# Attention with gated low-rank experts: orders in the slot of new weights, and probabilities of one or two key blocks written by four DMAs and read by one

## The reference

```python
xn = layernorm(x)
q = rmsnorm((xn @ Wq.T) as 32 heads of 128) * q_norm_w
k = rmsnorm((xn @ Wk.T) as 8 heads of 128) * k_norm_w
v = (xn @ Wv.T) as 8 heads of 128
scores = q @ k.T / sqrt(128)                 # 4 q heads share one k and v head
bias = where(rel > 0, -1e30, slope * rel)    # causal, with slopes by head
out = softmax(scores + bias) @ v
s = out @ Wo.T
g = silu(sum over 8 experts of the low-rank products, weighted by a softmax router)
y = x + s * g
```

## Time and profile before

| | |
|---|---|
| time, median of 3 runs | 741.79 us (741.38 to 743.2) |
| the profiled execution's own time | 743.02 us |
| its span in the trace | 741.2 us |
| TensorE busy | 720.8 us, 97% |
| VectorE, ScalarE, GpSimd busy | 600.6, 559.7, 335.6 us |
| DMA | 148.02 MB, mean 200 GB/s |
| granted TensorE clock | 0.998 |

### The profile page before, as it was taken

One profiled execution on the slowest core, in us unless ns is written; L12 is line 12 of the kernel. 1 busy time (PEld: TensorE's weight loads), 2 busy tenths in 40 slices (PEclk: granted clock), 3 DMA queues, 4 the chain that ended last, 5 costly groups with the idle time before them and its releaser, 6 DMA issues.

```text
span 741.2 us, 14630 instructions
## 1 busy us (share of the span) xinstructions
PE 720.8 (97%) x3741; PEld 605.4 (82%) x3741; DVE 600.6 (81%) x1490; ACT 559.7 (76%) x1440; POOL 335.6 (45%) x320
## 2 busy tenths in 40 slices
PE   8899999999999999999999999999999999999997
PEld 7787878878788888888888888888888887888776
DVE  6857798678886889787986889777986979878985
ACT  4566888587877877777886978778887768769873
POOL 4223434454434543545444543346326434445556
PEclk9999999999999999999999999999999999999999
DMA  8015968687685778868686786958787785867761
GB/s 304 1 30 140 274 170 235 194 239 224 172 267 160 223 203 229 242 158 254 183 231 198 229 241 173 280 141 232 214 229 217 191 264 147 232 196 204 205 191 72
DMA packets 214773, 148.02 MB, mean 200 GB/s; under 512 B 48992, under 2 KB 205536, under 8 KB 214624
## 3 DMA queue, kind: packets, MB, share of 16 engines
q1 hardware_dynamic: 184224, 130.39, 60.7%
q10 hardware_dynamic: 30528, 17.38, 8.9%
HBM read 85.84 MB, written 61.87 MB: 199 GB/s over the span
## 4 chain that ended last, share of the span: by engine, by line
PE 62%; DMA 10%; DVE 9%; issue 7%; ACT 6%; SPq 2%; POOL 2%; ACTq 1%; DVEq 0%; POOLq 0%
PE out_ps L1363 6%; PE qkv_ps L1363 5%; PE out_ps L1365 5%; PE qkv_ps L1364 5%; PE out_ps L1364 5%; PE qkv_ps L1365 5%; DMA x_sb<-turning 5%; PE score_ps L1363 4%; PE score_ps L1365 3%; PE score_ps L1364 3%; PE mix_ps L1363 3%; PE mix_ps L1365 3%; PE mix_ps L1364 3%; DMA turning<-squared 3%; PE turn_ps L1364 2%
## 5 line engine op out<-in xcount | busy, mean ns | idle before, releaser
L589 POOL TENSOR_TENSOR pt_lo<-x_sb,pt_hi 128x512 fp32r<-128x512 f32 x129 | 164.2, 1296 | 257.5 <-ACT pt_hi L795 257.5
L720 ACT ACTIVATE probs<-probs,neg_max 128x128 f32<-128x128 f32 (+3 forms) x256 | 142.1, 559 | 33.3 <-DVE neg_max L1018 32.1
L1018 DVE CUSTOM_DVE_ANT_0 probs<-score_ps,cst,slope 128x128 f32<-128x128 f32 (+3 forms) x256 | 131.0, 543 | 20.0 <-PE score_ps L1365 19.1
L728 ACT ACTIVATE probs<-probs,recip 128x128 f32<-128x128 f32 (+3 forms) x252 | 126.1, 549 | 8.0 <-DVE recip L1025 8.0
L795 ACT ACTIVATE pt_hi<-x_sb 128x512 fp32r<-128x512 f32 x153 | 86.6, 623 | 50.6 <-issue 31.7
L1363 PE MATMUL qkv_ps<-w_hi,xt_hi 128*128 128x256 f32 (+1 forms) x364 | 118.8, 326 | 2.4 <-DVE xt_lo L961 1.5
L1364 PE MATMUL qkv_ps<-w_lo,xt_hi 128*128 128x256 f32 (+1 forms) x364 | 118.4, 325 | 0.0
L1365 PE MATMUL qkv_ps<-w_hi,xt_lo 128*128 128x256 f32 (+1 forms) x364 | 118.0, 324 | 0.0
L1363 PE MATMUL out_ps<-wo_hi,o_hi 128*128 128x512 f32 x252 | 102.5, 407 | 0.8 <-DVE o_lo L1063 0.6
L1039 DVE STREAM_TRANSPOSE squared<-probs 128x256 f32<-128x256 f32 (+3 forms) x124 | 100.4, 810 | 0.1
L579 POOL TENSOR_TENSOR inv_rms<-sums,minus_half 128x5 f32<-128x5 f32 x64 | 76.9, 1202 | 50.1 <-DVE sums L1077 50.1
(11 more groups left out here) (203 smaller groups left out, 1630.3 us busy)
## 6 DMA issues: line engine op xcount, KB each, us to landing
qk_moved<-turning_qk SPq DMA_DIRECT2D x60, 320.0 KB, 3.4
turning_qk<-qk_squared ACTq DMA_DIRECT2D x212, 80.0 KB, 2.2
turning<-squared SPq DMA_DIRECT2D x120, 128.0 KB, 2.4
x_sb<-turning SPq DMA_DIRECT2D x30, 512.0 KB, 5.2
w_raw<-wqkv SPq DMA_DIRECT2D x32, 384.0 KB, 5.0
turning<-squared SPq DMA_DIRECT2D x120, 96.0 KB, 2.1
x_sb<-turning SPq DMA_DIRECT2D x30, 384.0 KB, 4.2
turning<-squared SPq DMA_DIRECT2D x128, 64.0 KB, 2.0
```

The lines of the kernel that those rows point to most:

```text
L589: nc.gpsimd.tensor_tensor(by_quad(pt_lo, j), moved_block(t, j), by_quad(pt_hi, j).bitcast(F32), ALU.subtract).then_inc(pt_lo_by_pool, 1)
L720: nc.scalar.activation(probs[:, h, 0:n], probs[:, h, 0:n], ACT.Exp, bias=neg_max[:, h:h + 1], scale=-1.0, accum_out=total[:, h:h + 1]).the ...
L728: nc.scalar.activation(to[:, h, 0:n], probs[:, h, 0:n], ACT.Copy, scale=recip[:, h:h + 1]).then_inc(probs_ready, 1)
L1018: nc.vector.tensor_tensor_reduce(probs[:, h, 0:n], score_bank(t, h), cst[:, C_DIST + SEQ - n:C_DIST + SEQ], slope[:, h:h + 1], HUGE, ALU.a ...
```

## The change

Four orders change, and one way through DRAM.

TensorE's `project_new` takes chunks 0 to 2 first, with `w_hi` and then with `w_lo`, and then chunk 3 with both; before, all four chunks with `w_hi` came first. The part of VectorE for the same slot (`w_slot`) makes the third `w_lo` ahead of the second reciprocals, and `turned_qk_lo` (q_lo and k_lo of the next unit) ahead of the first `square_probs`. The latter two are exchanged in slot t = 2 of the prologue too, there alone. In the last group's slot 5, GpSimd makes its block of `pt_lo` of unit 3 ahead of `inverse_rms`, as it did in the other groups.

The probabilities of a unit with one or two key blocks are laid out without a gap between the two pairs of heads, written by four DMAs once both pairs are there, and read by one. Units with three or four key blocks are moved as before. The counts that others wait for (`WRITTEN`, `MOVED`) follow.

```diff
-WRITTEN = counter([16 * QUADS] * BLOCKS)
-MOVED = counter([32] * BLOCKS)
+WRITTEN = counter([16 * QUADS] * BLOCKS), counter([0, 0, 16 * QUADS, 16 * QUADS] * BATCH)
+MOVED = counter([16, 16, 32, 32] * BATCH)
...
+        squared_whole = squared[:, :, :, :].rearrange("p k s n -> p k (s n)")
...
+        def moved_whole(t):
+            return moved[t % 2].rearrange("p q s n -> p q (s n)")[:, :, 0:keys_of(t) * P]
+
         def moved_block(t, j):
+            if keys_of(t) <= 2:
+                return moved_whole(t).rearrange("p q (s n) -> p q s n", s=2)[:, :, :, j * P // 2:(j + 1) * P // 2]
             return moved[t % 2][:, :, :, j * P // 2:(j + 1) * P // 2]
...
             def move(g, t, u, soon=False):
...
+                if keys_of(t) <= 2:
+                    if soon and u is not None:
+                        sp.wait_ge(qk_lo_ready, K_AND_Q_LO(g, u, 0))
+                        read_qk(g, u)
+                    write_all_probs(g, t)
+                    if u is not None and not soon:
+                        read_qk(g, u)
+                    sp.wait_ge(probs_written[0], WRITTEN[0](g, t, 16 * QUADS))
+                    sp.dma_start(moved_whole(t), turning[t % 2, :, :, 0:2 * n].rearrange("q p n -> p q n")).then_inc(probs_moved, 16)
+                    return
                 write_probs(g, t, 0)
...
+            def write_all_probs(g, t):
+                n = keys_of(t) * P
+                sp.wait_ge(probs_squared, TWO(g, t, 2))
+                for q in range(QUADS):
+                    sp.dma_start(turning[t % 2, q, :, 0:n].rearrange("(k r) n -> r k n", k=QUADS),
+                                 squared_whole[q * QUAD:(q + 1) * QUAD, :, 0:n]).then_inc(probs_written[0], 16)
...
@@ gpsimd, slot
-                if t % BLOCKS == W_SLOT and here(t + 3, left):
+                if t % BLOCKS == W_SLOT:
                     turned_lo(g, t - 2)
                 if here(t + 2, left):
                     inverse_rms(g, t + 2)
                 if t % BLOCKS == W_SLOT and here(t + 3, left):
                     split_w(g + 1, range(W_DVE, KC))
-                elif t % BLOCKS == W_SLOT:
-
-                    turned_lo(g, t - 2)
...
@@ vector, w_slot
                 reciprocals(g, t, 0)
+                split_w(g + 1, range(W_DVE - 1, W_DVE))
                 reciprocals(g, t, 2)
-                split_w(g + 1, range(W_DVE - 1, W_DVE))
                 normalize_q(g, t + 2)
                 square_both(g, t + 2)
+                turned_qk_lo(g, t + 1)
                 square_probs(g, t, 0)
-                turned_qk_lo(g, t + 1)
                 square_probs(g, t, 2)
...
@@ vector, slot
+                if t == 2:
+
+                    turned_qk_lo(g, t + 1)
                 if here(t, left):
                     square_probs(g, t, 0)
-                if here(t + 1, left):
+                if here(t + 1, left) and t > 2:
                     turned_qk_lo(g, t + 1)
...
@@ tensor, project_new
+                first, last = range(0, KC - 1), range(KC - 1, KC)
+                for chunks in (first, last):
+                    for to, cols, _ in parts:
+                        if chunks is first and to is parts[1][0]:
+                            pe.wait_ge(k_norm_ready, ONE(g, t - 1, 1))
+                            pe.wait_ge(v_lo_ready, ONE(g, t - 1, 1))
+                        for c in chunks:
                             pe.wait_ge(w_hi_done, (g + t // BLOCKS) * KC + (c + 1))
+                            pe.matmul(to, xt_hi[:, c, rows], w_hi[:, c, cols], start=c == 0, stop=False)
+                            pe.matmul(to, xt_lo[:, c, rows], w_hi[:, c, cols], start=False, stop=False)
+                    for c in chunks:
...
...
```

More of the change, by code:

```diff
@@ L468, in move @@
                                      qk_squared[q * QUAD:(q + 1) * QUAD, :, :]).then_inc(qk_written, 16)
+                if keys_of(t) <= 2:
[8 more added lines that the diff above has]
+                    return
                 write_probs(g, t, 0)
-                if soon:
+                if soon and u is not None:
                     sp.wait_ge(qk_lo_ready, K_AND_Q_LO(g, u, 0))
@@ L476, in move @@
                 for pair in range(2):
-                    sp.wait_ge(probs_written[pair], WRITTEN(g, t, 16 * QUADS))
+                    sp.wait_ge(probs_written[pair], WRITTEN[pair](g, t, 16 * QUADS))
                     sp.dma_start(to[:, :, pair, 0:n],
                                  turning[t % 2, :, :, pair * n:(pair + 1) * n].rearrange("q p n -> p q n")).then_inc(probs_moved, 16)
+            def write_all_probs(g, t):
[4 more added lines that the diff above has]
+                                 squared_whole[q * QUAD:(q + 1) * QUAD, :, 0:n]).then_inc(probs_written[0], 16)
             def write_probs(g, t, pair):
@@ L789, in moved_hi @@
             def moved_hi(g, t):
-                act.wait_ge(probs_moved, MOVED(g, t, 32))
+                act.wait_ge(probs_moved, MOVED(g, t + 1, 0))
                 if t > 0:
@@ L846, in end @@
                 for pair in range(2):
-                    act.wait_ge(probs_written[pair], WRITTEN(g, before, 0))
+                    act.wait_ge(probs_written[pair], WRITTEN[pair](g, before, 0))
                 normalize_probs(g, before, range(0, 2), late_probs)
@@ L1031, in square_probs @@
                 if t > 0:
-                    dve.wait_ge(probs_written[h // 2], WRITTEN(g, t, 0))
+                    dve.wait_ge(probs_written[h // 2], WRITTEN[h // 2](g, t, 0))
                 if t >= 2 and h == 2:
@@ L1037, in square_probs @@
                         dve.wait_ge(moved_lo_by_dve, DVE_BLOCKS(g, t - 1, 0))
-                blocks = squared[:, :, h // 2, :].rearrange("p k (j h n) -> p h j k n", j=QB, h=HPG // 2)
-                nc.vector.transpose(blocks[:, :, 0:keys_of(t), :, :],
+                if keys_of(t) <= 2:
+                    part = squared_whole[:, :, h // 2 * n // 2:(h // 2 + 1) * n // 2]
+                else:
+                    part = squared[:, :, h // 2, 0:n // 2]
+                nc.vector.transpose(part.rearrange("p k (j h n) -> p h j k n", j=keys_of(t), h=HPG // 2),
                                     probs[:, h:h + 2, 0:n].rearrange("p h (j k n) -> p h j k n", k=QUADS, n=QUAD)).then_inc(probs_squared, 1)
@@ L1408, in project_new @@
                 rows = slice(m * P, (m + 1) * P)
[L1409 to L1415, removed]
-                            pe.wait_ge(w_hi_done, (g + t // BLOCKS) * KC + (c + 1))
-                        pe.matmul(to, xt_hi[:, c, rows], w_hi[:, c, cols], start=c == 0, stop=False)
-                        pe.matmul(to, xt_lo[:, c, rows], w_hi[:, c, cols], start=False, stop=False)
@@ L1419, in project_new @@
[L1419 to L1427, removed]
+                parts = ((q_ps(t), slice(0, QW), q_ready), (qkv_ps[:, 1, 0:QKV - QW], slice(QW, QKV), kv_ready))
@@ new lines, in project_new @@
+                first, last = range(0, KC - 1), range(KC - 1, KC)
[5 more added lines that the diff above has]
+                        for c in chunks:
+                            pe.wait_ge(w_hi_done, (g + t // BLOCKS) * KC + (c + 1))
+                            pe.matmul(to, xt_hi[:, c, rows], w_hi[:, c, cols], start=c == 0, stop=False)
+                            pe.matmul(to, xt_lo[:, c, rows], w_hi[:, c, cols], start=False, stop=False)
+                    for c in chunks:
+                        if c < W_DVE:
+                            pe.wait_ge(w_lo_by_dve, (g + t // BLOCKS - 1) * W_DVE + (c + 1))
+                        else:
+                            pe.wait_ge(w_lo_by_pool, (g + t // BLOCKS - 1) * (KC - W_DVE) + (c - W_DVE + 1))
+                        for to, cols, done in parts:
+                            product = pe.matmul(to, xt_hi[:, c, rows], w_lo[:, c, cols], start=False, stop=c == KC - 1)
+                            if c == KC - 1:
+                                product.then_inc(done, 1)
```

## The result

| | before | after |
|---|---|---|
| median of 4 runs | 741.59 us (741.07 to 743.20) | 747.12 us (745.71 to 748.09) |
| profiled execution, its own time | 743.02 us | 745.71 us |
| its span | 741.2 us | 743.9 us |

The changed kernel takes 1.0076 times as long, with a 95% interval from 1.0056 to 1.0096: it is **5.5 us slower**. I had forecast 740.3 us, and 738.2 to 742.3 as the range. In a later comparison, against 29 runs of the kernel before, the ratio was 1.0088 (1.0068 to 1.0109). The profiled execution is the quickest of its four, and the one of the kernel before is near the slowest of its four, so the two traces show only 2.7 us of the loss.

The account below looks back on a forecast made before the run. TensorE, busy 720.8 of 741.2 us, was taken as the bound. Gains of 2.3 us (slots of new weights) and 0.2 (tail) less 1.0 (prologue) gave 1.5 off the 741.79 median: 740.3 us, range 738.2 to 742.3.

Parts of the forecast that it names:

- TensorE's new order: In project_new on new weights: the wait for w_hi before the fourth chunk goes; w_lo and k_lo are late next.
- what the place can give: Stalls from project_new's start to the next scores, summed over seven groups: at most 7.0 us to win.
- VectorE's new order: In the slot of new weights: q_lo and k_lo first; second transpose and bias come 0.38 us earlier in the third group.
- the term of -2.3 us: Gain in the slots of new weights: six groups by 0.38 us plus 0.05 for the fifth.
- a remaining wait for `neg_max`: At the last head of the next scores: TensorE waits about 0.7 us in the third group, little in the fifth.
- The DMAs of narrow units: Probabilities of units with one or two key blocks: no cost in the loop, 1.0 us lost in the prologue.
- Tail: After the last writes: unit 6's probabilities wait less for unit 5's writes, 0.2 us won; GpSimd's new order wins nothing.
- GpSimd's new order in the last group's slot 5: In the tail: mix of unit 3 comes forward, but VectorE blocks and o_lo come as before; worth nothing.
- A: Rival: reads are cheap or relieve queues, so the prologue's 1.0 us isn't lost: 739.3, down to 737.8 us; chance 0.33.
- B: Rival: all stalls in the slots of new weights go and nothing replaces them: 735.6 us; chance 0.03.
- C: Rival, slower: the prologue's lone read of unit 1 lands far later, 3.1 us lost, 742.4 us; chance 0.08.
- D: Rival: the exchange of orders is worth nothing because ScalarE, not VectorE, sets the bias too: 742.6 us; chance 0.06.

Follow-up runs that it names:

- e1: The kernel before with only the DMA part (four writes, one read for narrow units), all orders as before: 741.86 us, ratio 1.0022.
- e6: The kernel before with only VectorE's copy of the factor moved behind the norm of k: 739.03 us, ratio 0.9982.
- e2: The changed kernel with the old DMA way, keeping all four new orders: 744.58 us, ratio 1.0056 to the kernel before.
- e12: The changed kernel itself, measured again: 746.04 us, ratio 1.0088 to the kernel before.
- e3: The changed kernel with VectorE's copy of the factor moved from behind the addition to behind the norm of k: 742.19 us, ratio 1.0010.
- e5: The changed kernel with the factor's copy behind the norm of k and the first pair transposed ahead of q_lo: 737.60 us, ratio 0.9960.
- e7: The changed kernel with the early factor copy, first pair transposed ahead of q_lo, and the old DMA way: 736.85 us, ratio 0.9951.
- e8: The changed kernel with the factor's copy at its place but made by a reduction: 742.21 us, ratio 1.0016.
- e10: Repeat of e5, the changed kernel with both moves and the new DMAs: 738.66 us, ratio 0.9978.
- e11: Repeat of e7, the changed kernel with both moves and the old DMA way: 738.57 us, ratio 0.9967.
- both moves: On the changed kernel: the factor's copy moved behind the norm of k, and the first pair transposed ahead of q_lo; ratios 0.9951 to 0.9978.
- e9: The kernel before with the early factor copy and TensorE's new order of project_new, all else as before: 740.49 us, ratio 1.0012.

## Why the prediction was wrong, by its steps

**TensorE's new order: right in its mechanism.** No wait for `w_hi` in any group, and the projects' loss went from 7.0 to 1.4 us. Chunk 3's `w_lo` cost TensorE a wait of 0.10 us in the first group and none later; GpSimd began at 275.54, as soon as ScalarE's `w_hi` was there. But the 5.6 us aren't all the order's. The 7.0 that I took as what the place can give are those of one execution, 743.02 us, 1.2 above the median; with TensorE's old order e1's trace has 4.4 and e6's 2.9. And where TensorE is late at the scores, the other engines gain on it: the projects lose 1.4 in all three traces with both holds in every group (the changed kernel, e2, e12), and 2.0 to 2.8 in those with fewer (e3 to e5, e7, e8, e10, e11).

**VectorE's new order: this step failed.** The sum was "`q_lo` 0.57, `k_lo` 0.26, first transpose 0.59", then "everything behind it comes 0.38 us earlier, the bias too". It gave each instruction the duration that it had at its old place. Two of them had it only because GpSimd wasn't in an instruction at that moment. `q_lo` moved into GpSimd's `w_lo`: 1.06 instead of 0.57 us. With it the copy of the factor moved from 0.15 us ahead of GpSimd's `pt_lo` to 0.39 behind its start: 0.82 instead of 0.06. From the term of -2.3 us (six groups by 0.38), the place came to +3.1: of the 5.4 between, `q_lo` explains 0.46 to 0.49 in each of seven groups, 3.3, and the copies 5.1, together 8.4. So by these two traces the place would have won some 3 us more than my 2.3 without the holds. The other runs don't bear that surplus out. The four kernels with both moves are 1.8 to 4.0 us below the kernel before in the medians, with the early copy (e6: 1.8 us, not clear of noise) and the tail's 0.9 in it, and e7 is 2.2 us below e6 on the same chip. Measured from the start of the projection, ScalarE's `q_hi` came 1.04 us earlier in the third group than before (276.17 less 274.30, against 275.79 less 272.88), which my sum did not have; but TensorE, held in the groups before, had itself become late. How much the orders win without the holds thus stays open within some 2 us; what turned the sign are the two holds. I had named a remaining wait for `neg_max` of 0.7 us in the third group and little in the fifth. It was 1.18 and, in the fifth, 1.33:

```profile
454.60 0.45 PE L1391 MATMUL score_ps<-k_hi,q_hi 128*128 128x384 f32 x1 [1.33 <-DVE neg_max L1040]
```

**The DMAs of narrow units: within the range given.** In the loop they cost nothing that a trace shows. In the prologue, the chain of waits of the changed kernel, which answers to the earlier trace rows:

```profile
65.98 2.89 DMA turning<-squared
68.88 4.61 DMA x_sb<-turning
...
89.86 6.47 DMA w_raw<-wqkv
```

The lone 512 KB read took 4.61 us, where I took 4.2, and landed at 73.49, where I had 73.96 and before it was 72.95: 0.5 us lost instead of 1.0, because the last write was issued at 65.98 instead of 67.36; it took 2.89 where I took 2.4. VectorE's sums, 74.81 in the earlier trace rows, moved by the same 0.54:

```profile
75.35 0.83 DVE L1102 TENSOR_REDUCE sums<-squares 128x5 f32<-128x645 f32 x1 [2.28 <-ACT squares L805]
```

In e1, with the old orders, the read took 5.23 us and landed at 73.46. Single traces don't separate the two ways, though: in e7, with the old DMAs, unit 1's read landed at 73.46 as well, and in e2 at 72.95. Neither read comes near the estimate of 3.2 us by the Trainium skill's rule that the prediction cites ("DMA: Bandwidth & Descriptors", "Anatomy of one DMA"); the measurement decides. That section gives its fit for DMAs that GpSimd issues, and these are issued by SyncE. The scores of unit 5 came at 92.38 instead of 91.91.

**Tail: one term right in size, one wrongly put at nothing.** On TensorE the changed kernel is 2.58 us behind at the `mix` of 701.79 (704.37 now) and 2.15 behind at the `out` of 714.22 (716.37 now): 0.4 won, 0.2 forecast. The DMAs have about 0.3 of it: from the scores behind that `mix` to that `out` are 9.26 to 9.38 us in the kernels with the new DMAs and 9.39 to 9.65 in those with the old ones. GpSimd's new order in the last group's slot 5, which I had put at nothing, is worth 0.9 us more. Before, TensorE stood still for GpSimd's `pt_lo` of unit 3, and now it doesn't; before and after:

```profile
701.79 0.47 PE L1363 MATMUL mix_ps<-pt_hi,v_hi 128*128 128x512 f32 x1 [0.61 <-POOL pt_lo L589]
```
```profile
704.37 0.40 PE L1391 MATMUL mix_ps<-pt_hi,v_hi 128*128 128x512 f32 x1
```

From the start of the `out` ahead of this `mix` to the scores behind it, TensorE takes 6.40 to 6.42 us in the four kernels with the old order (before, e1, e6, e9) and 5.52 to 5.55 in all ten with the new one.

**The rivals.** A's condition, a read that lands as fast as before, didn't come true in this trace. B came half true (the stalls went) and its cost stood elsewhere. C put the loss of the slower side in the prologue's read; the sign was right, the place wrong. D came nearest in its result (742.6) for a false reason: the bias does hang on VectorE. No rival was made for an instruction that becomes longer where it is moved to, and so only 4 in 100 stood on the side that came.

## What to carry to other kernels

Before moving a VectorE instruction that reads two tensors of SBUF, or copies SBUF to SBUF, look at what GpSimd does at the new time and at the times of all that shifts with it; a copy of 128 x 5 numbers ahead of a critical instruction lost up to 1.1 us here. Look for such holds in durations, not in waits: compare the mean of one instruction by form between the two kernels, since the same count with more busy time is the sign. Take what a place can give from more than one trace: with TensorE's old order it lost 7.0, 4.4 and 2.9 us in three traces. Where the order can't be made safe, put transposes, reductions or operations on PSUM beside GpSimd, or use a reduction in place of a copy, as e8 did.

## What was unexpected of the hardware

A copy of 5 numbers per partition, 0.15 us by itself, took 1.22 us when it started 0.10 us behind a GpSimd instruction of 1.29 us, and 0.15 when it started 0.16 us ahead of one. So two instructions with no data in common decide by a quarter of a microsecond, seven times in an execution, over 1.1 us each. A reduction that writes the same numbers takes 0.14 us in the same place. It works the other way too: GpSimd's `inv_rms`, which takes 1.17 us in the median, took 1.61 or 1.62 beside VectorE's three `pt_lo` in four groups of the kernel before.
